# Adaptive block on one core: repeated rows read by token, with every engine's job order rewritten

## The reference

```python
y   = einsum(x, W[id]) + b[id]                       # a weight matrix chosen by each sequence's id
x   = x + layernorm((causal_linear_attention(y)) @ Wo * sigmoid(y @ G1 @ G2))
# part two, on the new x:
ctx = causal_ema(x, tau_ctx)
g   = x * sigmoid([x, ctx] @ Wg.T + bg)              # gated rows
m   = 0.5 + sigmoid(gelu(x @ Wn1.T) @ Wn2.T + bn2)   # 8 modulations per token
tr  = [causal_ema(g * m[..., d], tau[d]) for d in range(8)]     # eight decays
t   = sum_d tr[d] * softmax(blend)[d]                # blend per decay and feature
z   = layernorm((gelu(x @ Wsoma.T) * sigmoid(t @ Wtemp.T)) @ Wout.T)
out = x + bitlinear_ffn(z)                           # ternary weights, rows rounded to 8 bits, 1024 inner
```

## Time and profile before

| | |
|---|---|
| median of 3 runs | 710.37 us (710.12 to 710.71) |
| time of the profiled execution | 707.44 us |
| its span, first to last instruction | 705.5 us |
| TensorE busy | 642.1 us, 91% |
| TensorE weight loads busy | 472.1 us, 67% |
| VectorE busy | 549.7 us, 78% |
| ScalarE, GpSimd busy | 302.4 us, 309.2 us |
| mean granted TensorE clock | 0.960 |
| chain that ended last | TensorE 76%, VectorE 10%, DMA 9%, issue 3% |

### The profile page before, as it was taken

How to read it: one execution, slowest core, us unless ns; L and a number is a source line. 1 busy time by engine, 2 the same in 40 slices (tenths; PEclk the granted TensorE clock), 3 DMA queues, 4 the chain that set the end, 5 groups by cost and what they waited for, 6 DMA issues and landing times.

```text
span 705.5 us, 15004 instructions
## 1 busy us (share of the span) xinstructions
PE 642.1 (91%) x5766; PEld 472.1 (67%) x5766; DVE 549.7 (78%) x1068; ACT 302.4 (43%) x632; POOL 309.2 (44%) x313
## 2 busy tenths in 40 slices
PE   5689689999999999999999999999999999976653
PEld 3457467767777777778777777877786777764331
DVE  7789775878787778778797878787887978876864
ACT  4183334453544543534445444445344444533211
POOL 1260642435364726446362627272554626441222
PEclk9699899999999999999999999999999999999786
DMA  8411122215251634242341525152433325153322
GB/s 315 151 46 61 39 68 70 69 21 87 71 96 37 85 73 82 75 54 67 93 85 38 100 76 89 42 81 69 88 74 48 76 43 87 37 98 61 70 46 59
DMA packets 77034, 53.36 MB, mean 76 GB/s; under 512 B 57251, under 2 KB 69795, under 8 KB 76323
## 3 DMA queue, kind: packets, MB, share of 16 engines
q1 hardware_dynamic: 76676, 51.85, 35.3%
q10 hardware_dynamic: 288, 0.57, 0.3%
HBM read 35.48 MB, written 8.53 MB: 62 GB/s over the span
## 4 chain that ended last, share of the span: by engine, by line
PE 76%; DVE 10%; DMA 9%; issue 3%; POOL 1%; ACT 0%; POOLq 0%; SPq 0%; ACTq 0%; DVEq 0%
PE ps L475 69%; PE ps L478 7%; DMA B<-g_rows 5%; DMA g_rows<-G 2%; DVE B L905 2%; DVE EB L911 1%; DVE HP L908 1%; DMA HQ<-HM 1%; DVE EB L905 1%; DVE EB L908 1%; DVE FH L914 1%; DMA TT<-bpack 0%; DVE X L908 0%; DVE ZN L911 0%; DVE BN L1082 0%
## 5 line engine op out<-in xcount | busy, mean ns | idle before, releaser
L905 DVE TENSOR_TENSOR B<-B,BLGS 128x1024 f32<-128x1024 f32 x64 | 99.4, 1592 | 19.0 <-DMA B<-g_rows 18.8
L1207 POOL TENSOR_SCALAR HP<-HP,FT 128x1024 f32<-128x1024 f32 x32 | 41.2, 1289 | 149.2 <-DVE FT L908 149.2
L475 PE MATMUL ps<-WQ,YT 128*128 128x512 f32 (+1 forms) x256 | 88.1, 488 | 0.9 <-ACT YT L735 0.9
L905 DVE TENSOR_TENSOR EB<-ps,C 128x512 f32<-128x512 f32 x128 | 79.2, 680 | 8.2 <-PE ps L475 8.2
L475 PE MATMUL ps<-X1T,W 128*128 128x256 f32 x320 | 80.7, 383 | 1.5 <-DVE CT L1035 1.2
L905 DVE TENSOR_TENSOR HP<-FH,ps 128x512 f32<-128x512 f32 x64 | 42.4, 685 | 45.6 <-ACT FH L735 45.4
L475 PEld LDWEIGHTS ps<-WQ,YT 128*128 128x128 f32 x256 | 48.2, 190 | 36.1 <-issue 30.2
L475 PEld LDWEIGHTS ps<-X1T,W 128*128 128x128 f32 x320 | 58.3, 190 | 9.3 <-DVE CT L1035 2.0
L475 PE MATMUL ps<-FW,ZQ 128*128 128x512 bf16 x256 | 61.9, 386 | 0.0
L1160 POOL TENSOR_TENSOR X<-X,B 128x256 f32<-128x256 f32 x32 | 25.4, 797 | 67.6 <-DMA X<-x 67.6
L735 ACT ACT_TABLE_LOAD x40 | 51.3, 1283 | 2.3 <-PEq L1302 1.6
...
## 6 DMA issues: line engine op xcount, KB each, us to landing
B<-g_rows SPq DMA_DIRECT2D x32, 512.0 KB
XT<-xT SPq DMA_DIRECT2D x8, 512.0 KB, 3.8
...
```

The lines of the kernel that those rows point to most:

```text
L475: return e0.matmul(o, l, r, start=start, stop=stop, skip_group_check=True)
L905: return e0.tensor_tensor(o, x, y, op)
L1207: e0.tensor_scalar(HP[:, s, :], HP[:, s, :], FT[:, s, 2:3], MAGIC, ALU.mult, ALU.add).then_inc(g["hx"], 1)
```

## The change

Five edits go together.

1. The order of the 128 partitions becomes token, then r (4 i + r). `gr` reads with the 32 rows outermost and the four repeats inside. `diff`, `low` and `taurep`, the tables that depend on the order, follow.
2. `mr` is one transfer instead of four, and semaphore counts follow.
3. `BLGS` is read by a DMA (`blg` on SP) from the blends in DRAM. The four ScalarE copies go. `gr` waits for `uw` alone, and no longer for the copies and for `ubl`; `b4` waits for the new transfer.
4. `HM` is no buffer of its own: it lies over `HP`, in the slot that it is made from, so there are two. `hm` no longer waits for the transposes. In its place `fs` waits, before it writes `HP`, for the transpose of the chunk two before. `IDB` and its copy go.
5. The job tables of all five engines are new. The set of jobs is the same but for `blg`.

```diff
             def gr(c):
                 e.wait_ge(t["ema"], c - 1)
-                e.wait_ge(a["blg"], 4)
-                e.wait_ge(d["ubl"], 16)
+                e.wait_ge(d["uw"], 16)
                 e.wait_ge(d[f"gw{s}"], 16 * (c // 2 + 1))
-                e0.dma_start(B4[:, s, 0, :, :]..., GS[s].rearrange("i q c -> i (q c)").unsqueeze(0).to_broadcast([4, 32, NJ * CH]))
+                e0.dma_start(B4[:, s, 0, :, :]..., GS[s].rearrange("i q c -> i (q c)").unsqueeze(1).to_broadcast([32, 4, NJ * CH]))
...
+            def blg(n):
+                e.wait_ge(d["uw"], 16)
+                e0.dma_start(BLGS[:, :], US.rearrange("(r i) c -> r (i c)", i=2).unsqueeze(0).to_broadcast([32, 4, 2 * CH])).then_inc(d["blg"], 16)
...
-                for r in range(4):
-                    e0.dma_start(MODT[32 * r:32 * r + 32, s, :]..., MS[s, :, :, :, r, :].rearrange("j q i n -> i (j q) n"))
+                e0.dma_start(MODT[:, s, :]..., MS[s].rearrange("j q i r n -> (i r) (j q) n"))
...
             def fs(c):
-                    e.wait_ge(g["hm"], c - 1)
+                    e.wait_ge(d[f"hq{s}"], 16 * (c // 2))
...
             def hm(c):
-                e.wait_ge(d["hq0"], 16 * ((c + 1) // 2))
-                e.wait_ge(d["hq1"], 16 * (c // 2))
-                e0.tensor_scalar(HM[:, :], HP[:, s, :], -MAGIC, 1.0, ALU.add, ALU.mult)
+                e0.tensor_scalar(HM[:, s, 0:1024], HP[:, s, :], -MAGIC, 1.0, ALU.add, ALU.mult)
```

Of the tables, the stretches that matter most. VectorE, beginning of the period (k = 2 makes it unit 0 for `gt`, `tab2`, `modv`, `ae`):

```diff
-    ("em", 2, -2), ("tab2", 1, -2), ("b4", 2, -5), ("fin", 2, -10), ("wred", 1, 0), ("modv", 1, -2), ("gt", 1, -2), ("ae", 1, -2),
-    ("fs", 2, -8), ("fr", 2, -8), ("em", 2, -1), ("og", 2, -2), ...
+    ("em", 2, -2), ("b4", 2, -5), ("gt", 1, -2), ("rot", 1, 3), ("tab2", 1, -2), ("fs", 2, -8), ("fin", 2, -10), ("em", 2, -1),
+    ("og", 2, -2), ("fr", 2, -8), ("wred", 1, 0), ("on", 2, -2), ("modv", 1, -2), ("ae", 1, -2), ...
```

TensorE, end of the head, and SP, end of the head:

```diff
-    ("proj", 5), ("ktr", 4), ("xtr", 2), ("xtr", 3), ("qtr", 4), ("wsum", 2), ("soma", 1), ("ema", 0), ("gate", 2), ("e", 4), ("h1", 1), ("wg", 1),
+    ("proj", 5), ("xtr", 2), ("ktr", 4), ("xtr", 3), ("qtr", 4), ("wsum", 2), ("soma", 1), ("e", 4), ("h1", 1), ("ema", 0), ("wg", 1), ("gate", 2),
...
-    ("ffw", 2), ("mw", 0), ("uw", 0), ("ubl", 0), ("gw", 0), ("gr", 0), ("xin", 4), ("gw", 1), ("mr", 0),
+    ("gw", 0), ("uw", 0), ("gr", 0), ("ubl", 0), ("mw", 0), ("blg", 0), ("xin", 4), ("gw", 1), ("load", 3), ("mr", 0),
```

SP and VectorE near the end:

```diff
-    ("mw", 1, -1), ("gw", 2, -2), ("gr", 2, -2), ("mr", 1, -1), ("gw", 2, -1), ("hq", 2, -6), ("gr", 2, -1), ...
+    ("mw", 1, -1), ("gw", 2, -2), ("gw", 2, -1), ("gr", 2, -2), ("mr", 1, -1), ("gr", 2, -1), ...
...
-    ("ub", 1, -1), ("sg", 1, -2), ("b4", 2, -2), ("bn2", 1, -2), ("zc", 2, -4), ("zc", 2, -3), ("zn", 1, -2), ("b4", 2, -1), ...
+    ("b4", 2, -2), ("sg", 1, -2), ("fs", 2, -5), ("b4", 2, -1), ("bn2", 1, -2), ("zc", 2, -4), ("zc", 2, -3), ("zn", 1, -2), ...
```

More of the change, by code:

```diff
@@ L43 @@
-    ("proj", 5), ("ktr", 4), ("xtr", 2), ("xtr", 3), ("qtr", 4), ("wsum", 2), ("soma", 1), ("ema", 0), ("gate", 2), ("e", 4),
-    ("h1", 1), ("wg", 1),
+    ("cond", 0), ("cond", 1), ("proj", 0), ("proj", 1), ("ktr", 0), ("ktr", 1), ("qtr", 0), ("qtr", 1), ("e", 0), ("e", 1), ("o", 0),
+    ("low", 0), ("proj", 2), ("proj", 3), ("o", 1), ("gate", 0), ("qtr", 2), ("wo", 0), ("wo", 1), ("low", 1), ("wsum", 0), ("xtr", 0),
+    ("qtr", 3), ("ktr", 2), ("ktr", 3), ("xtr", 1), ("wsum", 1), ("e", 2), ("cond", 2), ("h1", 0), ("wg", 0), ("soma", 0), ("mod", 0),
@@ L45 @@
+    ("gate", 1), ("o", 2), ("e", 3), ("gtr", 0), ("wo", 2), ("proj", 4), ("o", 3), ("low", 2), ("gtr", 1), ("wo", 3), ("u", 0),
+    ("proj", 5), ("xtr", 2), ("ktr", 4), ("xtr", 3), ("qtr", 4), ("wsum", 2), ("soma", 1), ("e", 4), ("h1", 1), ("ema", 0), ("wg", 1),
+    ("gate", 2),
 )
 PE_PERIOD = (
-    ("ktr", 2, 1), ("qtr", 2, 1), ("cond", 1, 1), ("dn", 2, -8), ("mod", 1, -1), ("ztr", 2, -5), ("gu", 2, -6), ("o", 2, 0),
-    ("ema", 2, -3), ("e", 2, 1), ("gtr", 2, -2), ("wo", 2, 0), ("proj", 2, 2), ("gu", 2, -5), ("gtr", 2, -1), ("ttr", 1, -2),
@@ L49 @@
-    ("dn", 2, -7), ("o", 2, 1), ("u", 1, -1), ("low", 1, 1), ("wo", 2, 1), ("temp", 1, -2), ("proj", 2, 3), ("wsum", 1, 1),
-    ("xtr", 2, 0), ("ktr", 2, 2), ("wout", 2, -4), ("xtr", 2, 1), ("wout", 2, -3), ("qtr", 2, 2), ("soma", 1, 0), ("gate", 1, 1),
-    ("ema", 2, -2), ("e", 2, 2), ("wg", 1, 0), ("h1", 1, 0), ("ztr", 2, -4),
+    ("cond", 1, 1), ("mod", 1, -1), ("ktr", 2, 1), ("gu", 2, -6), ("qtr", 2, 1), ("o", 2, 0), ("ema", 2, -3), ("dn", 2, -8),
+    ("gtr", 2, -2), ("e", 2, 1), ("ztr", 2, -5), ("gtr", 2, -1), ("wo", 2, 0), ("proj", 2, 2), ("ttr", 1, -2), ("wsum", 1, 1),
@@ L52 @@
+    ("gu", 2, -5), ("o", 2, 1), ("low", 1, 1), ("u", 1, -1), ("wo", 2, 1), ("temp", 1, -2), ("xtr", 2, 0), ("dn", 2, -7),
+    ("proj", 2, 3), ("wout", 2, -4), ("ktr", 2, 2), ("qtr", 2, 2), ("wout", 2, -3), ("xtr", 2, 1), ("ema", 2, -2), ("soma", 1, 0),
+    ("wg", 1, 0), ("h1", 1, 0), ("gate", 1, 1), ("e", 2, 2), ("ztr", 2, -4),
 )
 PE_TAIL = (
-    ("ktr", 2, -5), ("qtr", 2, -5), ("cond", 1, -2), ("dn", 2, -14), ("mod", 1, -4), ("ztr", 2, -11), ("gu", 2, -12), ("o", 2, -6),
-    ("ema", 2, -9), ("e", 2, -5), ("gtr", 2, -8), ("wo", 2, -6), ("proj", 2, -4), ("gu", 2, -11), ("gtr", 2, -7), ("ttr", 1, -5),
@@ L56 @@
[L56 to L67, removed]
@@ new lines @@
+    ("wo", 2, -6), ("ttr", 1, -5), ("mod", 1, -4), ("ktr", 2, -5), ("gtr", 2, -8), ("proj", 2, -4), ("e", 2, -5), ("gu", 2, -11),
+    ("temp", 1, -5), ("dn", 2, -13), ("qtr", 2, -4), ("gtr", 2, -7), ("gate", 1, -2), ("o", 2, -5), ("ktr", 2, -4), ("proj", 2, -3),
+    ("wo", 2, -5), ("wout", 2, -10), ("wout", 2, -9), ("e", 2, -4), ("dn", 2, -12), ("cond", 1, -1), ("xtr", 2, -6), ("xtr", 2, -5),
+    ("u", 1, -4), ("o", 2, -4), ("qtr", 2, -3), ("soma", 1, -3), ("h1", 1, -3), ("wg", 1, -3), ("mod", 1, -3), ("ztr", 2, -10),
@@ new lines @@
+    ("ztr", 2, -9), ("dn", 2, -11), ("wo", 2, -4), ("ktr", 2, -3), ("gu", 2, -10), ("ema", 2, -8), ("ema", 2, -7), ("e", 2, -3),
+    ("gtr", 2, -6), ("gu", 2, -9), ("ttr", 1, -4), ("o", 2, -3), ("low", 1, -1), ("gtr", 2, -5), ("temp", 1, -4), ("wo", 2, -3),
+    ("proj", 2, -2), ("proj", 2, -1), ("xtr", 2, -4), ("u", 1, -3), ("gate", 1, -1), ("xtr", 2, -3), ("wout", 2, -8), ("wout", 2, -7),
+    ("qtr", 2, -2), ("h1", 1, -2), ("soma", 1, -2), ("ktr", 2, -2), ("mod", 1, -2), ("wg", 1, -2), ("ktr", 2, -1), ("ztr", 2, -8),
@@ new lines @@
+    ("e", 2, -2), ("gu", 2, -8), ("dn", 2, -10), ("gtr", 2, -4), ("qtr", 2, -1), ("o", 2, -2), ("e", 2, -1), ("ema", 2, -6),
+    ("ema", 2, -5), ("ztr", 2, -7), ("wo", 2, -2), ("o", 2, -1), ("ttr", 1, -3), ("gtr", 2, -3), ("wo", 2, -1), ("temp", 1, -3),
+    ("gu", 2, -7), ("wout", 2, -6), ("wout", 2, -5), ("xtr", 2, -2), ("u", 1, -2), ("xtr", 2, -1), ("dn", 2, -9), ("h1", 1, -1),
+    ("soma", 1, -1), ("wg", 1, -1), ("mod", 1, -1), ("ema", 2, -4), ("ztr", 2, -6), ("gtr", 2, -2), ("gtr", 2, -1), ("gu", 2, -6),
@@ L71 @@
+    ("dn", 2, -8), ("ztr", 2, -5), ("ema", 2, -3), ("dn", 2, -7), ("ttr", 1, -2), ("u", 1, -1), ("temp", 1, -2), ("gu", 2, -5),
+    ("wout", 2, -4), ("ema", 2, -2), ("wout", 2, -3), ("ema", 2, -1), ("ttr", 1, -1), ("temp", 1, -1), ("ztr", 2, -4), ("gu", 2, -4),
+    ("dn", 2, -6), ("ztr", 2, -3), ("wout", 2, -2), ("wout", 2, -1), ("gu", 2, -3), ("dn", 2, -5), ("dn", 2, -4), ("ztr", 2, -2),
+    ("ztr", 2, -1), ("gu", 2, -2), ("dn", 2, -3), ("gu", 2, -1), ("dn", 2, -2), ("dn", 2, -1),
 )
 ACT_HEAD = (
[4 rows of a table removed]
[4 rows of a table added]
@@ L290, in build @@
         d = sems("dma", "ids cpk thb wq wpk bgb blb ubl xt cw" + "".join(f" ff{i}" for i in range(3))
[L291 removed]
+                 + "".join(f" x{j}" for j in range(NJ)) + "".join(f" st{i}" for i in range(6)) + " uw blg mw0 mw1 mr0 mr1 gw0 gw1 gr0 gr1 hq0 hq1")
         t = sems("pe", "wsum cond proj lo gate qtr ktr e smm o wo xtr h1 mod wg soma gtr u ema ttr temp wout ztr gu dn")
[L293 to L294 removed]
+        a = sems("act", "lo tg sin p2 sp tab ex yt th vg qT kT ot x1t h1 mt wgt sm g tk tt tp zq fh")
+        v = sems("dve", "h1 eps rot red hb la1 p1 la3 la px mx wsm ws1 ws2 wq fw rq em ss og bn mv "
                  "on ctx modv ae gt ub b4 sg bn2 mv2 z1 z2 z3 z4 z5 zm f0 hp r1 r2 r3 r4 fq fin")
@@ L456, in _ @@
                     uw(n)
+                elif job == "blg":
+                    blg(n)
                 elif job == "gw":
@@ L1259, in _constants @@
     parts = {
-        "ident": np.eye(P), "mask": (f >= p) * 1.0, "diff": np.maximum(f[:, :32] - p % 32, 0), "low": (f[:, :32] >= p % 32) * 1.0,
+        "ident": np.eye(P), "mask": (f >= p) * 1.0, "diff": np.maximum(f[:, :32] - p // 4, 0), "low": (f[:, :32] >= p // 4) * 1.0,
         "sub": (p // 32 == f[:, :4]) * 1.0,
@@ L1284 @@
         "taurow": np.tile(a["condB_tauraws"], 16)[:, None],
-        "taurep": np.repeat(a["condB_tauraws"].reshape(4, 2), 32, axis=0),
+        "taurep": np.tile(a["condB_tauraws"].reshape(4, 2), (32, 1)),
     }
```

52 lines of the change are left out of this document (19 added, 33 removed), and 114 rows, old and new, of tables (ACT_HEAD, ACT_PERIOD, ACT_TAIL, DVE_PERIOD).

## The result

The changed kernel takes 704.7 us (median of 5 runs, 704.01 to 707.1), the kernel before 710.12 us in the same session (5 runs, 708.6 to 710.71). The ratio is 0.9935, 95% interval 0.9914 to 0.9957. So it is faster, but by 5.4 us where the forecast said 20, and it lies 0.7 us outside the range. The profiled execution took 704.7 us with a span of 702.9, against 707.44 and 705.5 before.

A forecast was written before the change was run, and what follows sets the result against it. TensorE was taken to bound the kernel, busy 500.72 of 502 us in the middle, with gains only at the ends. Head 9, middle 0, tail 10 and 1 for the wait made 20 off 710.4: 690.4 us, range 681 to 704.

The forecast's parts named there:

- The cover is complete, so the price is 0.: Middle, 100 to 602 us: same TensorE work in another order, costing 0, plus up to 1.3 us for one wait.
- the one wait of the middle: Middle: TensorE's single wait, up to 1.3 us in 502 us, entered in the sum as 1 us gained.
- the middle slips: Rival, middle: rewritten tables make TensorE wait in each period, 0.7 us a period, 9 us in all, giving 699; chance 0.16.
- The read: `gr` on the path at both ends: 3.8 us instead of 9.4, about 5.5 us less each, DMA share above 0.5.
- In the middle it is worth nothing: Middle: the 28 other `gr` get 5.5 us shorter too, which brings no time.
- the read is not faster: Rival, `gr`: twelve DMA engines may stay idle; new orders still give most of head and tail, about 698; chance 0.06.
- The head: Up to `ema 0`: it starts at about 89.4 instead of 95.8; 9 us gained, between 4 and 11.
- The 86: Head: the time in us when VectorE gets to `b4 0`, from which `ema 0` at about 89.4 was worked out.
- The tail: End of the run: last rows arrive earlier, partly offset by VectorE's moved normalisation; 10 us gained, between 5 and 15.
- Both terms: Tail: last rows there 16.5 us earlier, less 6.5 us of normalisation that VectorE does afterwards.
- The rest: Single modulation transfer costed at nothing, ScalarE not missing the blend copies, slots at cost 0 with some 5.5 us to spare.
- the slower rival: Rival, shared slot: late `hq` stalls `fs` on VectorE, then TensorE; 2 us a period give 716; chance 0.09.

The follow-up runs named there:

- `xin` too: Changed kernel with two loads of `x` before `gw` in SP's period and `fin` before the second `b4` in VectorE's: 698.03 us, again 697.24 us.
- the three swaps together: Changed kernel with `xin` before `gw`, `fin` before the second `b4`, and `rq 2`, `rq 3` before `tab0` in VectorE's head: 698.6 us, ratio 0.9845.
- The last kernels: Changed kernel with `xin` and `fin` moved earlier: `tab0` before `em 1`, 695.37 us; then also `blend0` before `rk 2`, 692.93 us.

## Why the prediction was wrong

**The step that failed is the middle: "The cover is complete, so the price is 0."** The price was 11.8 us, and the 1 us that the sum had for the one wait of the middle did not come either. TensorE was full there before because of the order in which the others served it, not only because they had time to spare. VectorE had 7.8 us free in every period, but free time on average says nothing of the one moment at which a PSUM bank has to come free. I priced jobs by length and looked at none of the new neighbours in VectorE's table against the ring. The rival "the middle slips" is the case that came true, with its price too small (9 us) and its chance too low (0.16). It named "the tightest pair" and not which. The runs name it: with `fin` moved in front of the second `b4`, the middle is 5.7 us shorter and the period 38.66; with `xin` too, another 2.0 us and 38.52. That is less than the 38.60 of before, so the steady period is fully accounted for. 4 us of the middle remain (422.9 against 418.9, or 5.3 against the 417.6 of the old tables with the new read). They lie at its two ends: in the kernel with the three swaps together TensorE is idle for 2.0 us from 100 to 180 us and for 3.1 from 480 to 602, but for 0.7 only from 200 to 480. The waits in the last stretch are seven short ones behind different operations, none above 0.6 us, and no kernel here takes them apart. That part stays open.

**The read: right.** 3.9 us for 3.8, the DMA share far above 0.5, `gr -1` issued 1.4 us after `gr -2`. "In the middle it is worth nothing" is right for the old tables (1.0 us) and wrong for the new ones (15.1 us): there the modulations stand behind it in SP's order, and through them it is on the path. For the same reason my rival "the read is not faster", 698, was far off: 740.

**The head: a wrong path, 2.9 for 9.** The prediction let `em 3` start 5.9 us earlier and made `b4 0`, at 86, the last thing that `ema 0` waits for. Neither held. The jobs `wred 2`, `modv` and `ae` do stand behind `em 3` now, but `em 3` starts at 78.06, where it was 78.23:

```profile
78.23 2.47 DVE L905 TENSOR_TENSOR EB<-ps,C 128x512 f32<-128x512 f32 x4
```

VectorE came 6.0 us later to that stretch (its `tab2` starts at 71.83 instead of 65.80). 3.4 us of these it had lost by `em 2` (66.44 for 63.09). The other 2.7 are `gt 0`, which now stands in front of `tab2`, and the 1.97 us for which it waited for its input from ScalarE. I read the timeline from 65 us on and never looked at what the new tables do at 35 to 47 us: `blend0` starts at 41.50 instead of 37.10, and `rq 2` and `rq 3` beside it cost 4.2 us more than their 1.4. The last kernels bear this out in part: with both orders undone `em 3` starts 2.2 us earlier (75.67 for 77.84) and the median falls by 4.3 us.

Then the path. The 86 was given without its sum: VectorE had been free for `b4 0` at 88.6, and the three moved jobs still had to be done before it. It came at 89.57, after 0.64 us of waiting for the read of `BLGS`, and took 3.95 us. (`uw` was forecast to stay at 76.97 and came at 82.58, after the later `blend1`; `gr 0` followed at 83.97.) But `ema 0` did not wait for it. The last wait of TensorE before `ema 0` is that of `u 0` for `ae 0`, one of the three jobs that were moved. `u 0` before, then `u 0` and `ema 0` in the changed kernel:

```profile
85.89 0.62 PE L475 MATMUL ps<-G,AE 128*32 128x256 f32 x4
```

```profile
85.81 0.94 PE L480 MATMUL ps<-G,AE 128*32 128x256 f32 x4 [1.91 <-DVE AE L904]
97.19 1.07 PE L480 MATMUL ps<-B,ML 128*32 128x256 f32 x16
```

From 85.81 on TensorE works without a gap. What the head gained lies behind `u 0`: the 2.66 us that `ema 0` had waited are gone. `proj 5` took 4.18 us instead of 2.85 (the granted clock was 0.65 there, so part of it ran at 1.2 GHz, and 1.00 before), and `ema 0` with the matmul behind it took 1.8 instead of 3.2 (1.00 there, 0.61 before), which evens out. Every kernel here with the new tables and the new read has the same wait of 1.9 us for `ae 0`; no run moves `ae` back, so what that alone would give is not shown. The 2.9 us are no more than the read gives alone (4.0 under the old tables).

**The tail: right, 11.5 for 10.** The waits for `B` in it are nearly gone. SP's issues and the last two `b4` on VectorE:

```profile
644.42 1.21 SPq L405 DMA_DIRECT2D g_rows<-G  x2
647.92 0.58 SPq L412 DMA_DIRECT2D B<-g_rows  x1
...
649.30 0.55 SPq L412 DMA_DIRECT2D B<-g_rows  x1
```

```profile
651.70 3.21 DVE L904 TENSOR_TENSOR B<-B,BLGS 128x1024 f32<-128x1024 f32 x2 [0.20 <-DMA B<-g_rows]
655.44 1.27 DVE L904 TENSOR_TENSOR HP<-FH,ps 128x512 f32<-128x512 f32 x2
656.63 2.35 DVE L904 TENSOR_TENSOR B<-B,BLGS 128x1024 f32<-128x1024 f32 x2
658.90 0.76 DVE L1082 BATCH_NORM_STATS2 BN<-ps 128x6 f32<-128x256 f32 x2
```

The last `b4` no longer waits for its transfer, and the normalisation (658.90) follows it, as forecast. By the kernels with the old tables, 6.1 us come from the read (181.6 to 175.5) and 6.1 from the order (175.5 to 169.4). Counted from the start of TensorE's TAIL, the last `b4` comes 15.2 us earlier (16.5 forecast for its rows). From it on, the kernel takes 46.3 us where it took 42.6: 3.7 us more, and not my 6.5. Both terms were somewhat too large, and the difference came out near. What TensorE waits for most from 600 us on is now the transposes, 11.1 us in four waits (8.6 in two before).

**The rest: right.** The single transfer for the modulation, the blends and the slots are worth nothing that these kernels show. No wait of `fs` for a transpose appeared, so the slower rival had no case. TensorE's idle time was forecast at 20 us in the first 100 (measured 25.3) and at 25 in the last (23.1).
